# FP4 feed-forward and phazor convolution: the block scales of h computed on ScalarE, the shifts moved behind the next maxima, the sums ahead of the next up

## The chip, the cores and the metric

One core of a Trainium2 chip. The metric is the device time of one launch in microseconds (us). Engines are named as in the profile: PE (TensorE), ACT (ScalarE), DVE (VectorE), POOL (GpSimd), SP (SyncE).

## What is computed

x is 4 x 1024 x 128 in f32. With xn = layernorm(x) over the last axis, the result is

```
x + conv(xn) + ffn(xn)

conv:  y[t] = Re( gate * ( sum over s <= t of phazor^(t-s) * init * xn[s]  +  last * phazor^(t+1) ) )
ffn:   q(h) @ q(w_down).T   with  h = silu(q(xn) @ q(w_gate).T) * (q(xn) @ q(w_up).T)

q(v), blockwise over 16 elements of the last axis:
    scale = max( max|v| / 6, 1e-12 )
    q     = nearest of 0, .5, 1, 1.5, 2, 3, 4, 6 to |v|/scale, * sign(v) * scale
```

The hidden width is 352, so a row of h has 22 blocks and a row of xn has 8. The reference does the convolution by FFT; the kernel does it as a recurrence in time, one channel to a partition.

## The kernel before, in words

The 4096 rows are 32 tiles of 128 rows. Four tiles make a **group of x** g (8 groups), two tiles make a **pair** q (16 pairs, two to a group). x is quantised, transposed and convolved by group; h is made, quantised and multiplied by w_down by pair.

Every engine has a queue written out by hand, and the engines meet by semaphores only. The queues are in order: an instruction that waits holds all behind it. The names below are those of the code and of the rest of the text.

For pair q of h: PE does gate_tile for each tile (L769, one PSUM bank, so each gate waits for the silu of the tile before) and up_pair (L778, into slot q % 2 of ps_u). ACT does silu (L622). DVE then does product (L959), maxima of the blocks (amax_h, L963), the scales (L974), their inverses (L977) and the divide (L982), in place in PSUM. ACT takes the absolute value times 2^22 (big_h, L632). DVE rounds by two subtractions, shift_h (L987) and shift_back_h (L994, into hn). POOL multiplies by the scales (scale_h, L452, into hq), PE turns it (turn_h, L790), ACT copies it (copy_hT, L628), and PE sums x, the convolution and the product with w_down into ps_o (sum_parts L800 to L803, sum_down L811). ACT copies the sum out (copy_out, L636) and SP stores it.

For group g of x: ACT normalises four tiles (L590), DVE takes the maxima (x_amax, L945). From group 3 on they lie next to those of h of the even pair q = 2(g - 2), so that one instruction makes both kinds of scales (76 columns instead of 44). POOL divides (divide_x, L386), ACT makes big_x in two steps (L597, L602), POOL shifts, shifts back and scales (L391, L396, L401), PE turns the quantised x (turn_xq) and the plain xn (turn_xn), and ACT copies both (copy_xqT L615, copy_xnT L609). POOL multiplies xn by two tables (demodulate_re, demodulate_im, L424), DVE scans each (L1008: the real part in the even pair, the imaginary part in the odd one, in pair 1 and pair 14 both kinds as the code below says), and POOL multiplies the scanned states by two tables (modulate_re, modulate_im, L439, into y_re and y_im). Between the two groups of a batch entry ACT turns the state by four one-column activations (turn_state, L553 to L559). A scan reads a column that lies in the bank of the next pair's up, so it waits for the first tile of up_pair(q + 1).

Before the loop ACT has made the sine tables, has gone through copy_xnT(0) and the big values of w_down, and DVE has done the statistics of the first two groups of x; those of the other six follow the divide of pair 0 on DVE, and normalise(2) on ACT waits for them.

DVE's order in pair q was shift_h(q-1), shift_back_h(q-1), product(q), amax_h(q), x_amax, scales(q), inverses(q), divide_h(q), scan. The scales and the inverses count up one semaphore together (s_rc, two to a pair). up_pair(q) waits for the shift back of pair q - 2, whose slot it takes.

## Time and profile before

| | us |
|---|---|
| median of 3 runs | 149.05 (148.79 to 150.4) |
| the profiled execution, its time | 150.65 |
| the profiled execution, its span | 148.6 |
| DVE busy | 125.8 (85%) |
| POOL busy | 113.5 (76%) |
| PE busy | 112.2 (76%) |
| ACT busy | 94.3 (63%) |

The span reaches from the first to the last instruction of the execution that the profiler recorded; the time of the same execution also holds what lies around it, 2.05 us. The runs are timed without a profile. Busy time counts the instructions that work, not semaphores or waits. A row of the order of time has the start from the span's beginning, the length, the engine, the line of the code, the operation with what it writes and reads, how many like instructions are merged in it, and in brackets the idle time ahead of it, where there is any of note, with the engine and line that ended it.

### The profile page before, as it was taken

Reading aid. Unit: us, or ns where it says so; the run is one execution under the profiler, and the core shown is the slowest. Engines: PE = TensorE matmul, PEld = TensorE weight load, DVE = VectorE, ACT = ScalarE, POOL = GpSimd, SP = SyncE. Lnnn points to the kernel's source line nnn. Section 1 sums busy time; section 2 is a strip of 40 time slices with the busy share of each in tenths; the row PEclk is TensorE's granted clock in tenths of the full one; section 3 lists DMA queues with packets and bytes.
Section 4 is the critical chain, followed back from the end, with each engine's and each line's share of the span. In section 5 each row is a group of like instructions: output and inputs, shape, how many; then the busy total and the mean of one; then the engine's idle time right before and its main releaser. Section 6 shows DMA issues by size and latency. Waiting matters only on the chain. (4 is left out here: it accounts for less than half of the span.)

```text
span 148.6 us, 2137 instructions
## 1 busy us (share of the span) xinstructions
PE 112.2 (76%) x649; PEld 88.0 (59%) x649; DVE 125.8 (85%) x222; ACT 94.3 (63%) x197; POOL 113.5 (76%) x130
## 2 busy tenths in 40 slices
PE   4405988206867459998996999699979999985883
PEld 4305644103534448785885878486757868674873
DVE  0999939999599893899999999999999999999900
ACT  3866449993596548668886774888485456641422
POOL 3677865659959999989996999799799954935300
PEclk9965599855589999999999999999999999999599
DMA  5970000000000000100010010001001000101011
GB/s 152 295 273 0 0 2 0 0 0 2 2 4 0 0 0 0 71 0 4 0 71 0 0 71 7 0 2 71 0 4 46 24 0 0 71 4 67 3 35 35
DMA packets 2890, 4.90 MB, mean 33 GB/s; under 512 B 448, under 2 KB 832, under 8 KB 2880
## 3 DMA queue, kind: packets, MB, share of 16 engines
q1 hardware_dynamic: 2736, 4.77, 9.2%
q8 instruction: 5, 0.08, 0.2%
q14 instruction: 5, 0.04, 0.1%
q10 hardware_dynamic: 144, 0.00, 0.1%
HBM read 2.67 MB, written 2.10 MB: 32 GB/s over the span
## 5 line engine op out<-in xcount | busy, mean ns | idle before, releaser
L769 PE MATMUL ps_g<-wg_T,xq_T 128*128 128x352 f32 x64 | 27.7, 517 | 10.4 <-ACT silu L622 10.4
L811 PE MATMUL ps_o<-wd_T,hq_T 128*128 128x128 f32 x180 | 25.7, 280 | 0.0
L811 PEld LDWEIGHTS ps_o<-wd_T,hq_T 128*128 128x128 f32 x180 | 23.5, 199 | 0.0
L778 PE MATMUL ps_u<-wu_T,xq_T 128*128 128x352 f32 x64 | 23.0, 483 | 0.0
L622 ACT ACTIVATE silu<-ps_g 128x352 f32<-128x352 f32 x32 | 14.7, 460 | 12.9 <-PE ps_g L769 12.9
L452 POOL TENSOR_TENSOR hq<-hn,den 128x704 f32<-128x704 bf16 x15 | 20.8, 1387 | 2.0 <-PE ps_o L811 1.6
L632 ACT ACTIVATE big<-ps_u 128x704 bf16<-128x704 f32 (+1 forms) x17 | 12.2, 720 | 14.9 <-DVE ps_u L982 14.9
L769 PEld LDWEIGHTS ps_g<-wg_T,xq_T 128*128 128x128 f32 x64 | 10.5, 202 | 16.0 <-ACT silu L622 13.8
L790 PEld LDWEIGHTS ps_h<-ident,hq 128*128 128x128 f32 x96 | 12.6, 145 | 10.4 <-issue 5.3
L790 PE MATMUL ps_h<-ident,hq 128*128 128x128 f32 x96 | 16.2, 279 | 2.7 <-POOL hq L452 1.5
L628 ACT COPY hq_T<-ps_h 128x384 f32<-128x384 f32 x32 | 15.2, 474 | 4.4 <-PE ps_h L790 4.4
L959 DVE TENSOR_TENSOR ps_u<-silu,ps_u 128x704 f32<-128x704 f32 x16 | 14.2, 889 | 2.4 <-ACT silu L622 2.4
L439 POOL TENSOR_TENSOR y_re<-g_re,out_re 128x512 f32<-128x512 f32 x8 | 10.1, 1267 | 7.6 <-DVE g_re L1008 7.6
L987 DVE SCALAR_TENSOR_TENSOR ps_u<-big,ps_u 128x704 f32<-128x704 bf16 (+1 forms) x17 | 14.1, 835 | 1.5 <-ACT big L632 1.4
L982 DVE TENSOR_TENSOR ps_u<-ps_u,inv 128x704 f32<-128x704 f32 (+1 forms) x17 | 14.4, 855 | 0.6
L590 ACT ACTIVATE xn<-x_all,shift,rstd 128x128 f32<-128x128 f32 x32 | 13.6, 489 | 2.0 <-DVE shift L915 2.0
L963 DVE TENSOR_REDUCE ps_u<-ps_u 128x44 f32<-128x704 f32 x16 | 14.4, 899 | 0.5
L994 DVE SCALAR_TENSOR_TENSOR hn<-big,ps_u 128x704 bf16<-128x704 bf16 (+1 forms) x17 | 14.3, 843 | 0.5
L778 PEld LDWEIGHTS ps_u<-wu_T,xq_T 128*128 128x128 f32 x64 | 11.6, 199 | 5.0 <-issue 1.0
L800 PE MATMUL ps_o<-x_all,ident 128*128 128x128 f32 x60 | 12.2, 286 | 2.6 <-POOL y_im L439 1.9
L391 POOL TENSOR_TENSOR xt<-xbig,xv 128x512 f32<-128x512 f32 (+1 forms) x9 | 10.4, 1154 | 4.8 <-ACT xbig L602 4.8
L724 PE MATMUL ps_o<-ident 128*128 128x128 f32 x32 | 7.0, 408 | 9.4 <-ACT w_big L570 7.3
(145 smaller groups left out, 259.7 us busy)
## 6 DMA issues: line engine op xcount, KB each, us to landing
x_all<-x_in SPq DMA_DIRECT2D x8, 256.0 KB, 6.0
out<-x_all SPq DMA_DIRECT2D x7, 256.0 KB, 2.0
w_raw<-w_in SPq DMA_DIRECT2D x1, 560.0 KB, 5.5
out<-x_all SPq DMA_DIRECT2D x1, 128.0 KB, 1.7
out<-x_all SPq DMA_DIRECT2D x2, 64.0 KB, 1.5
par<-params_in ACTq DMA_DIRECT2D x1, 3.5 KB, 3.0
```

The costliest lines, as they stand in the source:

```text
L452: pool.tensor_tensor(hq_blocks(q), hn_blocks(q), pair_scales(den[q % 4]), ALU.mult).then_inc(s_hq, 1)
L622: act.activation(silu[q % 2][:, j, :], ps_g[:, 0:I], ACT.Silu).then_inc(s_silu, 1)
L628: act.copy(hq_T[t % 3][:, :], ps_h[:, 0:NCH * P]).then_inc(s_hTc, 1)
L769: pe.matmul(ps_g[:, 0:I], x_cols(t), wg_T[:, :], start=True, stop=True).then_inc(s_gate, 1)
L778: pe.matmul(slot(q)[:, j, 0:I], x_cols(q * PAIR + j), wu_T[:, :], start=True, stop=True).then_inc(s_up, 1)
L790: m = pe.transpose(ps_h[:, c * P:(c + 1) * P], hq[q % 3][:, j, CUT[c]:CUT[c] + P], ident[:, :])
L811: m = pe.matmul(o, hq_T[t % 3][:, c * P:(c + 1) * P], wd_T[:, c, :], start=False, stop=(c == NCH - 1))
L959: dve.tensor_tensor(in_slot(q), silu[q % 2][:, :, :], in_slot(q), ALU.mult).then_inc(s_h, 1)
L963: dve.tensor_reduce(maxima(q)[:, 0:HBP].rearrange("p (j b) -> p j b", b=HB), slot_blocks(q), X_AXIS, ALU.max, apply_absolute_value=True).t ...
L982: dve.tensor_tensor(slot_blocks(q, j0, j1), slot_blocks(q, j0, j1), pair_scales(inv[q % 2], j0, j1), ALU.mult).then_inc(s_hv, 1)
L987: dve.scalar_tensor_tensor(in_slot(q, j0, j1), big[q % 2][:, j0:j1, :], FLOOR, in_slot(q, j0, j1), ALU.max, ALU.subtract).then_inc(s_ht, 1)
L994: dve.scalar_tensor_tensor(hn[q % 3][:, j0:j1, :], big[q % 2][:, j0:j1, :], FLOOR, in_slot(q, j0, j1), ALU.max, ALU.subtract).then_inc(s_h ...
```

## The change

The scale of each block leaves DVE. ACT computes it in two activations: Relu(max * NUDGE/6 - TINY*NUDGE) into a new tile `above`, and Identity(above + TINY*NUDGE) into den, which together are the max of the two. They have semaphores of their own (s_above, s_den), and the inverses on DVE wait for s_den; s_rc now counts one to a pair. POOL sets two more constant columns.

On ACT the call scales(q) stands: for pair 0 behind big_down(); in even pairs behind turn_state and ahead of copy_xqT; in odd pairs behind copy_xnT and ahead of normalise. On DVE both shifts of the pair ahead move behind the maxima of the pair, ahead of the inverses. On POOL shift_back_x moves up to right behind shift_x, ahead of scale_h, and demodulate_re(g) moves from the end of the odd pair into the next even pair, ahead of modulate_im(g - 1). On PE up_pair(q + 1) moves from ahead of the sums of the pair to behind them, except for q = 0.

```diff
@@ DVE, the loop
             for q in range(NP):
                 g = q // 2
+                product(q)
+                amax_h(q)
+                if with_x(q):
+                    x_amax(g + 2, maxima(q)[:, X_COLS])
                 if q > 0:
                     shift_h(q - 1, 0, 0, PAIR)
                     shift_back_h(q - 1, 0, 0, PAIR)
-                product(q)
-                amax_h(q)
                 if q == 1:
                     scale_of_first_x(2)
-                if with_x(q):
-                    x_amax(g + 2, maxima(q)[:, X_COLS])
-                scales(q, with_x(q))
+                inverses(q, with_x(q))
                 divide_h(q)
@@ DVE, scales() becomes inverses()
-            def scales(q, x):
+            def inverses(q, x):
                 n = HBP + (XBG if x else 0)
-                dve.wait_ge(s_ham, q + 1)
+                dve.wait_ge(s_den, q + 1)
                 if x:
-                    g = q // 2 + 2
-                    dve.wait_ge(s_xam, g + 1)
-                    dve.wait_ge(s_xv, x_done(g - 1))
-                    dve.wait_ge(s_xq, x_done(g - 2))
-                dve.tensor_scalar(den[q % 4][:, 0:n], maxima(q)[:, 0:n], NUDGE / 6, TINY * NUDGE, ALU.mult,
-                                  ALU.max).then_inc(s_rc, 1)
-                dve.wait_ge(s_rc, 2 * q + 1)
+                    dve.wait_ge(s_xv, x_done(q // 2 + 1))
                 dve.reciprocal(inv[q % 2][:, 0:n], den[q % 4][:, 0:n]).then_inc(s_rc, 1)
@@ ACT, new
+            def scales(q):
+                n = HBP + (XBG if with_x(q) else 0)
+                act.wait_ge(s_ham, q + 1)
+                if with_x(q):
+                    g = q // 2 + 2
+                    act.wait_ge(s_xam, g + 1)
+                    act.wait_ge(s_xq, x_done(g - 2))
+                act.activation(above[:, 0:n], maxima(q)[:, 0:n], ACT.Relu, scale=NUDGE / 6,
+                               bias=neg_tiny_c).then_inc(s_above, 1)
+                act.wait_ge(s_above, q + 1)
+                if q >= 4:
+                    act.wait_ge(s_hq, q - 3)
+                act.activation(den[q % 4][:, 0:n], above[:, 0:n], ACT.Identity, bias=tiny_c).then_inc(s_den, 1)
@@ ACT, its places
             copy_xnT(0)
             big_down()
+            scales(0)
             big_h(0, 0, 0, PAIR)
...
                     if g % HALVES:
                         turn_state(g - 1)
+                    scales(q)
                     if g + 1 < NG:
                         copy_xqT(g + 1, 1, 0, GT)
...
                     if g + 1 < NG:
                         copy_xnT(g + 1)
+                    scales(q)
                     if g + 3 < NG:
@@ POOL
                     elif g > 0:
+                        demodulate_re(g)
                         modulate_im(g - 1)
                     if g > 0:
                         demodulate_im(g)
...
                         if g + 2 < NG:
                             shift_x(g + 2, 1, 0, GT)
+                            shift_back_x(g + 2, 1, 0, GT)
                     scale_h(q - 1)
                     if g == 0:
                         divide_x(2, 1, 0, GT)
                         demodulate_re(1)
                         shift_x(2, 1, 0, GT)
+                        shift_back_x(2, 1, 0, GT)
                     if g + 2 < NG:
-                        shift_back_x(g + 2, 1, 0, GT)
                         scale_x(g + 2, 1, 0, GT)
-                    if 0 < g < NG - 1:
-                        demodulate_re(g + 1)
@@ PE
-                if q < LAST:
-                    up_pair(q + 1)
+                if q == 0:
+                    up_pair(1)
                 if q in (0, 2):
                     turn_xq(q // 2 + 1, 1, 0, GT)
                 if q >= 2:
...
                     sum_parts(b, out_cols(b))
                     sum_down(b, out_cols(b))
+                if 0 < q < LAST:
+                    up_pair(q + 1)
```

## Rows read from the trace of the kernel before

**Rows 1.** Part 1 of the page: busy time, share and instructions of each engine.
```profile
PE 112.2 (76%) x649; PEld 88.0 (59%) x649; DVE 125.8 (85%) x222; ACT 94.3 (63%) x197; POOL 113.5 (76%) x130
```

**Rows 2.** Order of time on DVE, pairs 6 and 7: start, length, engine, line, operation.
```profile
74.99 0.89 DVE L959 TENSOR_TENSOR ps_u<-silu,ps_u 128x704 f32<-128x704 f32 x1
75.91 0.90 DVE L963 TENSOR_REDUCE ps_u<-ps_u 128x44 f32<-128x704 f32 x1
76.72 0.68 DVE L945 TENSOR_REDUCE ps_u<-xn 128x32 f32<-128x512 f32 x1
77.50 0.24 DVE L974 TENSOR_SCALAR den<-ps_u 128x76 f32<-128x76 f32 x1
77.77 0.63 DVE L977 RECIPROCAL inv<-den 128x76 f32<-128x76 f32 x1
78.43 0.90 DVE L982 TENSOR_TENSOR ps_u<-ps_u,inv 128x704 f32<-128x704 f32 x1
79.24 1.27 DVE L1008 TENSOR_TENSOR_SCAN g_re<-ps_u,turned,u_re 128x512 f32<-128x512 f32 x1
80.43 0.87 DVE L987 SCALAR_TENSOR_TENSOR ps_u<-big,ps_u 128x704 f32<-128x704 bf16 x1
...
82.14 0.89 DVE L959 TENSOR_TENSOR ps_u<-silu,ps_u 128x704 f32<-128x704 f32 x1
...
88.41 0.89 DVE L959 TENSOR_TENSOR ps_u<-silu,ps_u 128x704 f32<-128x704 f32 x1
```

**Rows 3.** Order of time on ACT, same stretch.
```profile
72.21 0.76 ACT L632 ACTIVATE big<-ps_u 128x704 bf16<-128x704 f32 x1 [0.46 <-DVE ps_u L982]
...
76.71 0.57 ACT L615 COPY xq_T<-ps_x 128x512 f32<-128x512 f32 x1
...
79.36 0.76 ACT L632 ACTIVATE big<-ps_u 128x704 bf16<-128x704 f32 x1 [1.30 <-DVE ps_u L982]
80.02 0.62 ACT L597 ACTIVATE xsq<-xv 128x512 f32<-128x512 f32 x1
...
81.30 0.44 ACT L622 ACTIVATE silu<-ps_g 128x352 f32<-128x352 f32 x1
...
84.29 0.89 ACT L590 ACTIVATE xn<-x_all,shift,rstd 128x128 f32<-128x128 f32 x2
```

**Rows 4.** Groups of ACT by form: count, then busy time and mean ns of one.
```profile
L556 ACT ACTIVATE turned<-g_re,turned,cos_t 128x1 f32<-128x1 f32 x4 | 1.5, 379 | 0.0
...
L602 ACT ACTIVATE xbig<-xsq,consts 128x256 f32<-128x256 f32 x2 | 1.0, 509 | 0.1
```

**Rows 5.** Order of time on POOL, same stretch.
```profile
74.56 1.28 POOL L439 TENSOR_TENSOR y_im<-g_im,out_im 128x512 f32<-128x512 f32 x1
...
77.02 1.39 POOL L452 TENSOR_TENSOR hq<-hn,den 128x704 f32<-128x704 bf16 x1
78.47 1.06 POOL L386 TENSOR_TENSOR xv<-xn,inv 128x512 f32<-128x512 f32 x1
```

**Rows 6.** Order of time on PE, same stretch: sums of two tiles, and what follows them.
```profile
76.81 0.38 PE L800 MATMUL ps_o<-x_all,ident 128*128 128x128 f32 x2
...
79.07 0.60 PE L745 MATMUL ps_x<-ident,xn 128*128 128x128 f32 x4
```

**Rows 7.** Order of time on DVE: inverses of pair 0, divides of pairs 2 and 15.
```profile
24.53 0.43 DVE L977 RECIPROCAL inv<-den 128x44 f32<-128x44 f32 x1
...
47.97 0.90 DVE L982 TENSOR_TENSOR ps_u<-ps_u,inv 128x704 f32<-128x704 f32 x1
...
137.77 0.96 DVE L982 TENSOR_TENSOR ps_u<-ps_u,inv 128x352 f32<-128x352 f32 x2
```

**Rows 8.** Order of time on ACT at the start: big_h(0) and copy_xnT(1).
```profile
27.95 0.74 ACT L632 ACTIVATE big<-ps_u 128x704 bf16<-128x704 f32 x1
...
39.57 1.07 ACT L609 COPY xn_T<-ps_x 128x512 f32<-128x512 f32 x1
```

**Rows 9.** Order of time on PE at the end: sum_parts(28).
```profile
138.08 0.77 PE L800 MATMUL ps_o<-x_all,ident 128*128 128x128 f32 x2 [0.72 <-issue]
```

More of the change, by code:

```diff
@@ L77, in build @@
         ident = sb("ident", [P, P])
-        consts = sb("consts", [P, 4])
+        consts = sb("consts", [P, 6])
+        above = sb("above", [P, HBP + XBG])
         steps = sb("steps", [P, GT + 1], I32)
@@ L202, in build @@
         s_ham = sem("h_amax_ready")
+        s_above = sem("h_scales_above_tiny")
+        s_den = sem("h_scales_ready")
         s_rc = sem("h_inverses_ready")
@@ L236, in build @@
         first_re, first_im, neg_turn = col(18), col(19), col(20)
-        base_c, quarter_c, round_c, unround_c = (consts[:, n:n + 1] for n in range(4))
+        base_c, quarter_c, round_c, unround_c, tiny_c, neg_tiny_c = (consts[:, n:n + 1] for n in range(6))
         X_COLS = slice(HBP, HBP + XBG)
@@ L317, in _ @@
             pool.memset(ident[:, :], 0.0).then_inc(s_idz, 1)
-            for c, value in ((base_c, BASE), (quarter_c, math.pi / 2), (round_c, ROUND), (unround_c, -ROUND)):
+            for c, value in ((base_c, BASE), (quarter_c, math.pi / 2), (round_c, ROUND), (unround_c, -ROUND),
+                             (tiny_c, TINY * NUDGE), (neg_tiny_c, -TINY * NUDGE)):
                 pool.memset(c, value).then_inc(s_const, 1)
@@ L382, in divide_x @@
                 else:
-                    pool.wait_ge(s_rc, 4 * g - 6)
+                    pool.wait_ge(s_rc, 2 * g - 3)
                 if g >= 3:
@@ L519, in whole_turns @@
             def whole_turns():
-                act.wait_ge(s_const, 4)
+                act.wait_ge(s_const, 6)
                 act.wait_ge(s_turns, 1)
@@ L964, in amax_h @@
                                   X_AXIS, ALU.max, apply_absolute_value=True).then_inc(s_ham, 1)
-            def scales(q, x):
+            def inverses(q, x):
                 n = HBP + (XBG if x else 0)
-                dve.wait_ge(s_ham, q + 1)
+                dve.wait_ge(s_den, q + 1)
                 if x:
-                    g = q // 2 + 2
-                    dve.wait_ge(s_xam, g + 1)
-                    dve.wait_ge(s_xv, x_done(g - 1))
-                    dve.wait_ge(s_xq, x_done(g - 2))
-                dve.tensor_scalar(den[q % 4][:, 0:n], maxima(q)[:, 0:n], NUDGE / 6, TINY * NUDGE, ALU.mult,
-                                  ALU.max).then_inc(s_rc, 1)
-                dve.wait_ge(s_rc, 2 * q + 1)
+                    dve.wait_ge(s_xv, x_done(q // 2 + 1))
                 dve.reciprocal(inv[q % 2][:, 0:n], den[q % 4][:, 0:n]).then_inc(s_rc, 1)
             def divide_h(q):
-                dve.wait_ge(s_rc, 2 * q + 2)
+                dve.wait_ge(s_rc, q + 1)
                 for j0, j1 in parts(q):
```

## The prediction

> **What bounds the kernel now.** I read the page's busy line first: DVE is the busiest engine at 85%, PE and POOL follow at 76%, ACT at 63% [rows 1]. A share over the whole span doesn't say which engine sets the pace of a stretch, so next comes DVE's own order of time over one group of x (two pairs, q=6 and q=7). Its instructions follow each other with no idle bracket, and the group takes 88.41 - 74.99 = 13.42 us [rows 2]. DVE is the bound there. The reader is to see the steps from start to start, because they are what an instruction costs in a full queue: product 0.92, maxima 0.81, maxima of x 0.78, scales 0.27, inverses 0.66 (with x), divide 0.81, scan 1.19, both shifts 1.71 (80.43 to 82.14) [rows 2]. Then ACT in the same stretch, for how late it comes with what DVE will now need [rows 3], then what POOL and PE do around it [rows 5, 6], and last the start and the end, where the engines hand one chain from one to the other [rows 7 to 9].
>
> **Part 1, the scale leaves DVE.** Sixteen tensor_scalar go, each worth 0.27 us (77.50 to 77.77). The reduction in front of it, 0.68 long, stepped 0.78 because the scale waited for its result; the one of 0.90 whose follower doesn't wait stepped 0.81 (75.91 to 76.72) [rows 2]. The shift that now follows doesn't wait either: another 0.1 to 0.2, taken as 0.1. So DVE alone would need 0.37 less per pair: an even pair with x 7.15 - 0.37 = 6.78, an odd one 6.27 - 0.37 = 5.90, a group 12.7 us. That is the whole gain on offer, about 16 x 0.37 = 5.9 us.
>
> **Part 2, its price on ACT.** Two dependent activations of 44 or 76 columns with a pointer bias take its place. The trace has none of this form. The nearest are 379 ns for one column with pointer scale and bias, and 509 ns for 256 columns with a bias alone [rows 4]. Reading between them gives about 0.35 each, and with the wait of the second for the first 0.75 us for both; the bounds are 0.5 (two of 0.25, if pointers cost less here than in the 379) and 0.95 (two of 0.45, between the two rows, and their hand-over). The Trainium skill, "ScalarE: Activation LUTs", Rules for kernel authors, budgets about 0.3 us plus 0.83 ns per element, an estimate of 0.67 to 0.73 for the two.
> The cover for it is the 1.7 us of both shifts, if ACT is free by then. ACT's queue is in order, and scales(q) stands behind silu, the hT copies and, in odd pairs, copy_xnT(g+1). So I follow ACT from the end of a divide.
>
> **Part 3, the new order on DVE moves ACT later.** Before, divide(q-1) was followed by scan and both shifts, and only then product(q): ACT's big_h(q-1), which starts when the divide ends, ran 2.8 us ahead of product(q) (79.36 against 82.14) [rows 2, 3]. Now only the scan lies between, and big_h(q-1) starts 1.1 us ahead. Everything behind it on ACT comes 1.7 us later against DVE, and scales(q) is one of those things.
> Odd pair with big_x (q=3, 5, 7, 9, 11), time 0 at the start of divide(q-1): the divide ends at 0.90; big_h starts at 0.93 and holds ACT 0.66. big_x needs divide_x, which stands on POOL behind scale_h(q-2); and scale_h(q-2) needs the shift back of that pair, which now ends only right before inverses(q-1), at about -0.6. scale_h 1.39 and divide_x 1.06 follow (77.02, 78.47) [rows 5]: xv is ready at about 1.95. So big_x starts at 1.95 and not at 1.6; its two activations step 1.28 (80.02 to 81.30); from silu(2q+2) to the end of copy_xnT are 2.99 (81.30 to 84.29) [rows 3]; the two new activations 0.75. The scales are ready at 7.0. DVE would be there at 0.81 + 1.19 + 0.92 + 0.81 + 1.71 = 5.44. It waits 1.5 us. A group is then 12.7 + 1.5 = 14.2 to 14.3 us, against 13.42: **0.8 us more per group**, not 0.7 less. With the scales at 0.5 and no wait for xv it would be 13.7, with 0.95 14.5; all are above 13.42.
> Even pairs: ACT has copy_out, two silu, two hT copies and, for odd g, the four activations of turn_state ahead of scales(q). From big_h(5) to their end it took 4.5 (72.21 to 76.71) [rows 3], 5.3 with the scales, where DVE needs from the divide's end 1.1 + 0.92 + 0.81 + 0.7 + 1.71 = 5.2. Nothing to speak of with x; without x (q=14, with turn_state) 0.7.
>
> **Part 4, POOL and PE.** POOL gets demodulate_re in front of modulate_im, so y_im, which ended 0.85 us after product(6) began (74.56 + 1.28 - 74.99) [rows 2, 5], comes at about 2.9 if POOL has no slack; in a longer group POOL has it (demodulate_re runs while DVE waits), y_im comes at about 1.4 and the sums start at 2.3. They now go ahead of up: 2.26 us of PE work (76.81 to 79.07) [rows 6] before up(q+1) starts, at 4.5 after product(q); its first tile, which the scan waits for, is there at 5.2 and the scan wants it at 5.6. Covered by 0.4 us; costed at nothing. On the last groups (q=12 on), where there is no big_x, gate(2q+2) comes behind sums and up and holds silu(2q+2) about as long as big_x did, so there is no gain there either. A wait placed on ACT holds silu, and with it the gate tiles.
>
> **Part 5, the start, where the change is dearest.** In pair 0 the inverses started at 24.53, and the moments and statistics of the late x followed the divide without a gap [rows 7]. Now inverses(0) needs scales(0), which ACT reaches behind silu(3), copy_xnT(0) and big_down, at 27.95, where big_h(0) began [rows 8]. With 0.75 the scales are there at 28.70 and inverses(0) starts at 28.75: **4.2 us later**, bounds 4.0 and 4.4. No shift stands in pair 0 to cover it. Moments, statistics, normalise(2), turn_xn(1), the gates of pair 2 all stand behind it, so the whole kernel moves by 4.2.
> Pair 1: scales(1) stands behind copy_xnT(1), which started at 39.57, and steps 0.85: 40.42 in the old clock [rows 8], scales ready at 41.2, divide at 41.65, scan at 42.45. The scan of before waited for up(2) as well, and began 2.0 earlier; the shifts of pair 1 then come behind product(2) in the new order. Carried through to divide(2), which was at 47.97 [rows 7], it is 1.7 more.
> Pairs 2 to 6: up(3) stands behind the first sums, which need y_im(0). By the same bookkeeping the scan of pair 2 waits 3.6 us for it and inverses(3) 1.2 for ACT, while waits of before go, so that little of it is net. From divide(2) to divide(6) I get 31.7 us against 78.43 - 47.97 = 30.5 [rows 2, 7]: 1.2 more, of which 0.8 is the group of pairs 5 and 6.
> Pairs 7 to 12: three more groups, 3 x 0.8 = 2.5. Pairs 13 to 15: the same path by ACT without big_x, with gate behind sums and up, 1.1. **The end:** the shift back of pair 14 ends only 0.46 ahead of divide(15), and POOL does scale_h(14) and modulate_im(7) behind it, 1.39 + 1.28 [rows 5], so y_im comes 2.2 after the divide's start; the sums of the last tiles want it, and began 0.3 after it (138.08 against 137.77) [rows 7, 9]. That is 1.9 later, of which I take 0.7 as got back further down, where PE and the hT copies wait for each other in turn: 1.2, bounds 0 and 2.
> **Sum:** 4.2 + 1.7 + 1.2 + 2.5 + 1.1 + 1.2 = 11.9 us on the profiled execution: span 148.6 to 160.5, its time 150.65 to 162.5. The median of the runs is 1.6 below the profiled execution's time, so against 149.05 the forecast is **161**.
>
> **The rivals.** (a) ACT is ready in time from pair 2 on: silu and copies move up into the idle that ACT has today (63% busy [rows 1]), and only the start pays. Then 4.2 + 1.7 + 1.2 less 13 x 0.37 = 4.8: +2.3, about 151. For it: ACT has idle time in each group. Against it: that idle lies ahead of big_h, on the wrong side of the chain counted in part 3.
> (b) The change works throughout, pair 0 too: DVE stays the bound and 5.9 less up to 1.2 at the end comes off: 143 to 145. It needs ACT free for scales(0) 4 us before its queue got there [rows 8]. The Trainium skill, "Perfetto Trace Analysis", Optimizing Scalar/DVE Operations, speaks for (b): with DVE saturated, "offloading some work to Scalar (or even GPSIMD) may make sense". The trace bears out the premise (no DVE idle over 13.42 us), not that ACT's queue gets there in time.
> (c) Slower still: the sums ahead of up stop the scan of every even pair because y_im stays late. If y_im comes at 2.9 in each group, up's first tile is at 5.85 instead of 5.6: 0.25 a group, plus up to 0.6 where the gate behind them comes later than big_x, over 5 groups: +4, 165. It decides only if POOL doesn't get back its slack.
> (d) It does something else than it says: Relu swaps ACT's table. Two reloads a pair, at anything near a microsecond each, would be over 20 us. The Trainium skill, "ScalarE: Activation LUTs", Table sets, lists relu as filler in every set; no run here shows it yet, but Square, Identity, Abs, Sin and Silu already run in this kernel without a swap between them.
>
> **How the numbers follow.** Forecast 0.78; (a) 0.08; (b) 0.04; (c) 0.09; (d) 0.01. The unknown costs of the forecast: the steady groups between +0.3 and +1.1 each (-2.5, +1), start 4.0 to 4.4, pairs 2 to 4 -1.5 to +1, the end -1.2 to +0.8. Together 155.5 to 163.5; the range reaches to (c)'s lower part and stops short of (a): 155 to 164. One per cent (1.5 us) is about what a measurement of this kernel can tell from no change: faster than that 0.04, within it 0.04, slower 0.92.
>
> **What would show it.** Step by step: DVE idle ahead of the inverses of pair 0, released by ACT's second activation, 4.2 us; ahead of those of odd pairs from 3 to 11, 1 to 1.5 us each, with copy_xnT right ahead of the scales on ACT; none in even pairs with x; starts of products two pairs apart 14.2 us; activations of 0.3 to 0.4 us. It is wrong if the inverses of odd pairs start right behind the shift back, or if the group is under 13.4 us; if the price is right and the place wrong, the idle stands ahead of the scans, with up as releaser, and (c) has it.

## The result, and the profile after

168.52 us median (167.46 to 169.68) against 149.44 for the kernel before beside it: ratio 1.127, 95% interval 1.116 to 1.139. The change makes the kernel slower by 19 us; the forecast was 12, to 161 us, with a range of 155 to 164. The direction and the price of the steady groups came out as worked. Three stretches were priced too low, and the cause of the largest miss was not in the sum at all. In this text a time is the median of all timed executions, while a ratio and its interval leave out executions in a slower state (among them one of 384.92 us of e5 and one of 168.34 us of e7).

The page of the changed kernel: span, busy times, and the group of the inverses from part 5.

```profile
span 167.4 us, 2167 instructions
...
PE 116.0 (69%) x649; PEld 91.0 (54%) x649; DVE 126.9 (76%) x206; ACT 102.2 (61%) x229; POOL 113.9 (68%) x132
...
L994 DVE RECIPROCAL inv<-den 128x44 f32<-128x44 f32 (+1 forms) x16 | 7.8, 487 | 14.7 <-ACT den L650 14.7
```

DVE is busy 1.1 us longer than before (126.9 against 125.8 [rows 1]), although the scales have left it, and idle 17.7 us longer (40.5 against 22.8). 14.7 us of the idle time are waits of the inverses for ACT: 4.36 in pair 0, 3.25 in pair 1, 0.60 in pair 3, 1.4 in each of pairs 5, 7, 9 and 11, and 0.57 and 0.30 in pairs 13 and 14.

The divides on DVE, order of time, pairs 4, 12 and 15; pairs 2 and 6 stand in fences below (57.91, 91.87), those of before in [rows 2, 7].

```profile
77.77 0.90 DVE L999 TENSOR_TENSOR ps_u<-ps_u,inv 128x704 f32<-128x704 f32 x1
...
133.35 0.90 DVE L999 TENSOR_TENSOR ps_u<-ps_u,inv 128x704 f32<-128x704 f32 x1
...
153.73 0.96 DVE L999 TENSOR_TENSOR ps_u<-ps_u,inv 128x352 f32<-128x352 f32 x2
```

Against the kernel before (whose divides of pairs 0, 4 and 12 began at 24.99, 65.01 and 117.80) the divide of pair 0 comes 3.8 us later, that of pair 2 9.9, of pair 4 12.8, of pair 6 13.4, of pair 12 15.6, of pair 15 16.0, and the end 18.8. The forecast had 4.2, 5.9, 6.3, 7.1, 9.6, 10.7 and 11.9. So the misses lie between pairs 0 and 2 (6.2 lost, 1.7 forecast), between pairs 2 and 4 (2.8 lost, 0.4 forecast) and at the end (2.8 lost, 1.2 forecast). From pair 4 to pair 15 it went the other way: the changed kernel lost 3.2 where 4.4 were forecast.

**The start.** DVE's order of time, from the inverses of pair 0 to the shift column, and POOL's beside it.

```profile
28.31 0.43 DVE L994 RECIPROCAL inv<-den 128x44 f32<-128x44 f32 x1 [4.36 <-ACT den L650]
28.77 0.90 DVE L999 TENSOR_TENSOR ps_u<-ps_u,inv 128x704 f32<-128x704 f32 x1
...
32.88 0.18 DVE L930 TENSOR_SCALAR rstd<-var 128x24 int32<-128x24 int32 x1
33.09 1.20 DVE L933 TENSOR_TENSOR tmp<-rstd 128x24 f32<-128x24 f32 x1
34.33 1.19 DVE L934 SCALAR_TENSOR_TENSOR tmp<-tmp,var 128x24 f32<-128x24 f32 x1
...
37.65 0.18 DVE L934 SCALAR_TENSOR_TENSOR tmp<-tmp,var 128x24 f32<-128x24 f32 x1
...
39.60 1.19 DVE L936 SCALAR_TENSOR_TENSOR rstd<-tmp,rstd 128x24 f32<-128x24 f32 x1
40.82 0.18 DVE L938 SCALAR_TENSOR_TENSOR shift<-mean,rstd 128x24 f32<-128x24 f32 x1
```

```profile
32.99 1.26 POOL L368 TENSOR_TENSOR in_re<-terms 128x512 f32<-128x512 f32 x1 [4.65 <-ACT terms L543]
34.21 1.26 POOL L369 TENSOR_TENSOR in_im<-terms 128x512 f32<-128x512 f32 x1
...
39.49 1.26 POOL L428 TENSOR_TENSOR u_im<-xn_T,in_im 128x512 f32<-128x512 f32 x1
```

The inverses wait 4.36 us for ACT, as forecast. The steps of the statistics that follow take 0.18 us up to 33.09. From there seven of the ten that are left take 0.65 to 1.20, and each of the seven ends 0.03 to 0.05 us after an instruction of POOL: 33.09 + 1.20 = 34.29 against 32.99 + 1.26 = 34.25, then 34.33 + 1.19 = 35.52 against 34.21 + 1.26 = 35.47. From the divide to the end of the shift column it is 41.00 - 28.77 = 12.2 us; before it was 32.52 - 24.99 = 7.5. The kernel before had shown it once, in the last step, which met POOL's first table:

```profile
31.04 0.18 DVE L913 SCALAR_TENSOR_TENSOR rstd<-tmp,rstd 128x24 f32<-128x24 f32 x1
31.26 1.26 DVE L915 SCALAR_TENSOR_TENSOR shift<-mean,rstd 128x24 f32<-128x24 f32 x1
...
31.22 1.26 POOL L364 TENSOR_TENSOR in_re<-terms 128x512 f32<-128x512 f32 x1 [2.48 <-ACT terms L539]
```

0.18 for the step that ran alone, 1.26 for the one that began 0.04 us after POOL's. The statistics had just missed the table work; 3.8 us later they lay under it. The Trainium skill, "SBUF — State Buffer", Who interferes with whom, has the rule: a DVE instruction with two inputs in SBUF and a GpSimd (POOL) instruction that reads SBUF contend for a shared port pair that one holds for its whole length, and the other is fully blocked. The trace agrees in every step above: the steps that began before POOL's instruction kept their 0.18 us (37.65 against 37.66 on POOL), those that began after it waited for its end.

The stretch counts as busy time of DVE, so it hides in the busy share; only the order of time shows it.

**The steady groups.** DVE, pairs 7 to 9, and ACT in the odd pair between.

```profile
87.18 0.87 DVE L982 TENSOR_TENSOR ps_u<-silu,ps_u 128x704 f32<-128x704 f32 x1
...
91.21 0.62 DVE L994 RECIPROCAL inv<-den 128x76 f32<-128x76 f32 x1
91.87 0.90 DVE L999 TENSOR_TENSOR ps_u<-ps_u,inv 128x704 f32<-128x704 f32 x1
92.67 1.27 DVE L1025 TENSOR_TENSOR_SCAN g_re<-ps_u,turned,u_re 128x512 f32<-128x512 f32 x1
...
98.81 0.43 DVE L994 RECIPROCAL inv<-den 128x44 f32<-128x44 f32 x1 [1.42 <-ACT den L650]
...
101.28 0.87 DVE L982 TENSOR_TENSOR ps_u<-silu,ps_u 128x704 f32<-128x704 f32 x1
```

```profile
93.81 0.63 ACT L601 ACTIVATE xsq<-xv 128x512 f32<-128x512 f32 x1 [0.25 <-POOL xv L390]
...
95.10 0.44 ACT L626 ACTIVATE silu<-ps_g 128x352 f32<-128x352 f32 x1
...
97.21 1.13 ACT L613 COPY xn_T<-ps_x 128x512 f32<-128x512 f32 x1
98.09 0.33 ACT L645 ACTIVATE above<-ps_u,consts 128x44 f32<-128x44 f32 x1
98.45 0.33 ACT L650 ACTIVATE den<-above,consts 128x44 f32<-128x44 f32 x1
98.69 0.86 ACT L594 ACTIVATE xn<-x_all,shift,rstd 128x128 f32<-128x128 f32 x2
```

The group, from one product to that two pairs on, takes 101.28 - 87.18 = 14.10 us (14.2 forecast, 13.42 before [rows 2]). In the even pair the inverses follow without idle; in the odd one they wait 1.42 us for den, the second activation on ACT, right behind copy_xnT. From the start of the first activation to the end of the second are 98.45 + 0.33 - 98.09 = 0.69 us (0.75 forecast).

**The first sums.** PE's windows (the columns are named in the first line) and the scan of pair 2.

```profile
core 0: us, PE busy (x) PEld busy (x) DVE busy (x) ACT busy (x) POOL busy (x), PEclk, DMA share, GB/s
59.44:63.83 4.39, 4.39 (x20) 4.39 (x21) 0.00 (x0) 0.91 (x3) 3.57 (x3) 0.50 0.01 4
```

```profile
57.91 0.90 DVE L999 TENSOR_TENSOR ps_u<-ps_u,inv 128x704 f32<-128x704 f32 x1
65.31 1.28 DVE L1025 TENSOR_TENSOR_SCAN g_re<-ps_u,turned,u_re 128x512 f32<-128x512 f32 x1 [6.50 <-PE ps_u L799]
```

The sums of tiles 0 and 1 take 4.39 us at a granted clock of 0.50; in steady pairs they take 2.3 [rows 6], and the same first sums of the kernel before took 2.34 (50.39 to 52.73) at 1.00. PE had worked 0.72 us in the 4.51 us ahead of them. up(3) stands behind them, and the scan waits 6.50 us for it, where 3.6 were forecast.

**The end.** POOL and PE behind the divide at 153.73.

```profile
153.44 1.38 POOL L456 TENSOR_TENSOR hq<-hn,den 128x704 f32<-128x704 bf16 x1 [3.35 <-DVE hn L1011]
154.78 1.27 POOL L443 TENSOR_TENSOR y_im<-g_im,out_im 128x512 f32<-128x512 f32 x1
```

```profile
156.14 0.77 PE L821 MATMUL ps_o<-x_all,ident 128*128 128x128 f32 x2 [0.37 <-issue]
```

ACT: copy_hT(28), and big_h(15) behind it.

```profile
155.81 0.48 ACT L632 COPY hq_T<-ps_h 128x384 f32<-128x384 f32 x1 [3.00 <-PE ps_h L811]
156.19 0.83 ACT L636 ACTIVATE big<-ps_u 128x352 bf16<-128x352 f32 x2
```

scale_h(14) and y_im come as worked, y_im ends at 156.05, 2.3 us after the divide's start. But hT(28) comes late too, and big_h(15) on ACT stands behind its copy: it begins 2.5 us after the start of the divide, where before it began 0.6 after it (138.34 against 137.77). From the start of the last divide to the end of the span are 13.7 us against 10.8. The first tile's sums ran at half clock in both kernels; those of the second (from 159.05) run at half clock only in the changed one. What that costs by itself no run separates.

### The profile page after: what moved, and what is told of

It is laid out like the page before. It is cut to its first block, busy times and chain, and to the rows that moved or that the text cites. A ratio compares the mean times of both kernels' runs of the same rounds, so it can differ in the third digit from the quotient of the medians.

```text
span 167.4 us, 2167 instructions
## 1 busy us (share of the span) xinstructions
PE 116.0 (69%) x649; PEld 91.0 (54%) x649; DVE 126.9 (76%) x206; ACT 102.2 (61%) x229; POOL 113.9 (68%) x132
## 4 chain that ended last, share of the span: by engine, by line
PE 22%; DVE 22%; issue 20%; POOL 18%; ACT 15%; DMA 2%; POOLq 0%; ACTq 0%; DVEq 0%
PE ps_g L790 6%; PE ps_o L832 4%; ACT xn_T L613 3%; PE ps_u L799 3%; POOL xt L400 3%; POOL xt L395 3%; ACT silu L626 3%; POOL y_re L443 3%; POOL hq L456 2%; DVE bn L912 2%; DVE ps_u L999 2%; POOL u_im L428 2%; DVE rstd L936 2%; PE ps_o L821 2%; DMA par<-params_in 2%
## 5 line engine op out<-in xcount | busy, mean ns | idle before, releaser
L790 PE MATMUL ps_g<-wg_T,xq_T 128*128 128x352 f32 x64 | 27.8, 518 | 13.7 <-ACT silu L626 13.5
L832 PE MATMUL ps_o<-wd_T,hq_T 128*128 128x128 f32 x180 | 27.3, 292 | 0.0
L832 PEld LDWEIGHTS ps_o<-wd_T,hq_T 128*128 128x128 f32 x180 | 25.2, 211 | 0.0
L790 PEld LDWEIGHTS ps_g<-wg_T,xq_T 128*128 128x128 f32 x64 | 11.0, 202 | 20.5 <-ACT silu L626 16.9
L636 ACT ACTIVATE big<-ps_u 128x704 bf16<-128x704 f32 (+1 forms) x17 | 12.2, 722 | 14.0 <-DVE ps_u L999 14.0
L811 PE MATMUL ps_h<-ident,hq 128*128 128x128 f32 x96 | 16.8, 287 | 4.8 <-POOL hq L456 3.3
L994 DVE RECIPROCAL inv<-den 128x44 f32<-128x44 f32 (+1 forms) x16 | 7.8, 487 | 14.7 <-ACT den L650 14.7
L594 ACT ACTIVATE xn<-x_all,shift,rstd 128x128 f32<-128x128 f32 x32 | 13.5, 482 | 8.8 <-DVE shift L938 8.8
L766 PE MATMUL ps_x<-ident,xn 128*128 128x128 f32 x32 | 5.3, 292 | 15.4 <-ACT xq_T L619 15.4
L1004 DVE SCALAR_TENSOR_TENSOR ps_u<-big,ps_u 128x704 f32<-128x704 bf16 (+1 forms) x17 | 14.2, 843 | 2.0 <-ACT big L636 2.0
L799 PEld LDWEIGHTS ps_u<-wu_T,xq_T 128*128 128x128 f32 x64 | 12.2, 208 | 4.9 <-issue 1.5
L1011 DVE SCALAR_TENSOR_TENSOR hn<-big,ps_u 128x704 bf16<-128x704 bf16 (+1 forms) x17 | 14.2, 842 | 0.5
L821 PE MATMUL ps_o<-x_all,ident 128*128 128x128 f32 x60 | 12.9, 300 | 2.4 <-POOL y_im L443 1.9
```

The costliest lines, as they stand in the source:

```text
L790: pe.matmul(ps_g[:, 0:I], x_cols(t), wg_T[:, :], start=True, stop=True).then_inc(s_gate, 1)
L799: pe.matmul(slot(q)[:, j, 0:I], x_cols(q * PAIR + j), wu_T[:, :], start=True, stop=True).then_inc(s_up, 1)
L811: m = pe.transpose(ps_h[:, c * P:(c + 1) * P], hq[q % 3][:, j, CUT[c]:CUT[c] + P], ident[:, :])
L821: pe.matmul(o, ident[:, :], x_all[:, t, :], start=True, stop=False)
L832: m = pe.matmul(o, hq_T[t % 3][:, c * P:(c + 1) * P], wd_T[:, c, :], start=False, stop=(c == NCH - 1))
L1004: dve.scalar_tensor_tensor(in_slot(q, j0, j1), big[q % 2][:, j0:j1, :], FLOOR, in_slot(q, j0, j1), ALU.max, ALU.subtract).then_inc(s_ht, 1)
```

## The experiments

All but e6 start from the changed kernel. The ratios compare with the kernel before, run beside each experiment on the same chip; the microseconds that a run is said to gain are, unless another run is named, against the 168.52 of the changed kernel, timed separately beside a kernel before of 149.44. The place of the first instructions in the span differs from one profile to the next (the inverses of pair 0 of e8 to e13, all but e11, begin at 23.94 to 25.83), so lengths are taken within one profile. "The scan waits for up" means that it waits for the first tile of the next pair's up on PE.

**e1: scales of pair 0 on DVE.**

```diff
@@ DVE, pair 0 alone
+                if q == 0:
+                    scales(q, with_x(q))
                 inverses(q, with_x(q))
@@ ACT
-            scales(0)
```

scales(q, x) on DVE is the tensor_scalar of the kernel before, counting up s_den.

> The changed kernel, with the scales of pair 0 alone made on DVE as before. Theory A (the late scales cost twice: DVE waits 4.4 us for ACT, and the statistics, pushed under POOL's table work, stretch from 7.5 to 12.2 us from divide to shift column, because DVE's small instructions on two SBUF operands wait for each POOL instruction to end): the divide of pair 0 is back at about 25, the shift column ends at about 32.5, and with PE idle for 7 instead of 15 us its granted clock is back at full before the first sums; together 8.5 to 11 us less than the changed kernel, 157.5 to 160. Rival R1 (the stretch of the statistics has another cause than when they run): 4.2 us less, about 164.

159.51 us, ratio 1.064 (1.052 to 1.075): 9 us less, in the range of theory A. The divide of pair 0 is back at 24.90 and that of pair 1 at 41.50 (50.05 in the changed kernel), so the start cost about twice its wait. The hoped-for clock was not there: the granted clock from 47 to 54 us, in which the first sums begin, is 0.50, and the scan of pair 2 still waits 5.4 us.

**e2: POOL waits for the statistics.**

```diff
@@ POOL
             first_state()
+            pool.wait_ge(s_stats, 2)
             in_tables()
```

> The changed kernel, but POOL waits for the late statistics before it makes the in tables; DVE's late start stays. Theory A (POOL's instructions hold DVE's small ones): every step of the statistics is 0.2 us again, from the divide of pair 0 to the end of the shift column 7.5 us as in the kernel before, at most 6.5 without the stretch of the last one; POOL's tables come later, so the whole gains only 2 to 4.5 us: 164 to 166.5. Rival R1 (ACT's table terms, or the semaphore hand-over, stretch them): the steps stay at up to 1.2 us and the time at 168.5 or above it.

161.56 us, ratio 1.082 (1.073 to 1.092), 7 us less from one added wait: more than theory A said, which had counted on a loss by POOL's later tables. DVE's late start stays (divide of pair 0 at 28.43), and the steps are short:

```profile
32.75 0.18 DVE L934 TENSOR_TENSOR tmp<-rstd 128x24 f32<-128x24 f32 x1
...
34.70 0.18 DVE L939 SCALAR_TENSOR_TENSOR shift<-mean,rstd 128x24 f32<-128x24 f32 x1
```

The shift column ends at 34.88 instead of 41.00: from the divide 6.45 us instead of 12.23. The rest of the gain shows at the scan of pair 2, which waits 5.2 us for up instead of 6.5. Nothing on ACT or in DVE's own semaphores was changed, so POOL's instructions were what held DVE.

**e3: all scales on DVE, the other moves kept.**

```diff
@@ DVE, every pair
+                scales(q, with_x(q))
                 inverses(q, with_x(q))
@@ ACT
-            every call of scales(q)
```

> The changed kernel with the scales of all pairs on DVE (right ahead of the inverses, so that nothing waits for them), all the other moves kept. Theory A (ACT's in-order queue makes the odd pairs wait): no idle ahead of the inverses, group of x 12.7 + 0.5 = 13.2 to 13.4 us, start as in the kernel before; 150 to 154. Rival R2 (the moves of the shifts and of up cost by themselves, through silu and gate): the group stays near 14 us, the idle moves to the product or the scan; 156 to 159.

157.07 us, ratio 1.049 (1.039 to 1.059). No inverses wait, the start is that of before (12.81 us from divide to divide of pairs 0 and 1 in both), and yet it is 8 us slower than before: rival R2 had the time (156 to 159) and the place.

```profile
67.56 0.90 DVE L1008 TENSOR_TENSOR ps_u<-ps_u,inv 128x704 f32<-128x704 f32 x1
68.51 1.28 DVE L1034 TENSOR_TENSOR_SCAN g_re<-ps_u,vec,u_re 128x512 f32<-128x512 f32 x1
...
75.15 1.28 DVE L1034 TENSOR_TENSOR_SCAN g_im<-ps_u,vec,u_im 128x512 f32<-128x512 f32 x1 [0.41 <-PE ps_u L796]
...
81.31 0.90 DVE L1008 TENSOR_TENSOR ps_u<-ps_u,inv 128x704 f32<-128x704 f32 x1
```

The group is 81.31 - 67.56 = 13.75 us. The scans of odd pairs now wait for up behind the sums (0.41 in pair 5, 0.55 in the next ones; pair 4 loses 0.14, 0.95 from divide to scan instead of 0.81), and the scan of pair 2 waits 7.0.

**e4: scales of the odd pairs ahead of silu(2q+3) on ACT.**

```diff
@@ ACT, odd pairs
                         copy_hT(2 * q - 4)
+                    scales(q)
                     if q < LAST:
                         silu_tile(2 * q + 3)
...
                         copy_xnT(g + 1)
-                    scales(q)
```

> The changed kernel with scales(q) of the odd pairs moved on ACT ahead of silu(2q+3), where ACT waits for the gate anyway. Theory A: the 1.4 us of idle ahead of the inverses of odd pairs goes, but big_h then waits behind the normalise, so the group falls from 14.1 to between 13.0 and 13.5; 3 to 5 us less, 163.5 to 165.5. Rival R2 (the odd pairs are held by something else of the new order): group above 13.8, time within 1.5 of 168.5.

165.05 us, ratio 1.103 (1.092 to 1.113): the time is in theory A's range, the group is not. The waits of the odd inverses from pair 3 on are gone, and the group goes from 14.1 to 13.76 us (76.32 to 90.08), where theory A named 13.0 to 13.5. The scans take over: that of pair 4 waits 0.3 us for up, that of pair 5 0.7, and those of pairs 7, 9 and 11 wait 1.07. Of the shorter wait of the inverses of pair 1 (0.30 instead of 3.25) little comes through: counted from the divide of pair 0, that of pair 4 is 1.2 us earlier.

**e5: up(3) ahead of the first sums.**

```diff
@@ PE
-                if q == 0:
-                    up_pair(1)
+                if q in (0, 2):
+                    up_pair(q + 1)
```

> The changed kernel, with up_pair(3) alone back ahead of the first sums on PE. Theory A (the 6.5 us that the scan of pair 2 waits are those sums, which wait for y_im(0) and then run at half the granted clock, and gate(8) stands behind up(3) too): the wait of that scan falls under 1 us; the inverses of pair 3 then wait for ACT, which needs the divide of x from POOL first, so 2.5 to 3.5 us less in all: 165 to 166. Rival R3 (all of the wait is net loss): 6 us less, 162.5. Rival R4 (the wait is of no account, the den of pair 3 ends later anyway): within 1 of 168.5.

167.10 us, ratio 1.119 (1.110 to 1.128): 1.4 us less, between the ranges of theory A and of rival R4. The same kernel in one more execution, for its waits:

> The kernel of e5 once more for one look at its waits. As in e5: the scan of pair 2 waits under 1 us, the inverses of pair 3 for ACT, span about 165.

Span 163.6, time 165.55. The scan of pair 2 waits for nothing, the inverses of pair 3 wait 3.2 us for ACT, and the divide of pair 4 comes at 74.88 instead of 77.77. So of a wait of 6.5 us 1.4 (by the medians) to 2.9 (by this divide) were net loss.

**e6: the kernel before with up behind the sums.** The same move on PE as in the change, nothing else.

```diff
@@ PE
-                if q < LAST:
-                    up_pair(q + 1)
+                if q == 0:
+                    up_pair(1)
...
                     sum_down(b, out_cols(b))
+                if 0 < q < LAST:
+                    up_pair(q + 1)
```

> The kernel before with the move on PE alone: up_pair(q+1) behind the sums for q > 0. Theory A: nothing in the steady groups (DVE still 13.42 a group), but the scan of pair 2 waits for the first sums, some 5 to 6 us where it waited for nothing, of which later waits of the kernel before (3.3 us) give part back: 151.5 to 154.5. Rival R3: the scans of the steady pairs wait too, 0.5 us or more in each, and the time is over 156.

155.29 us, ratio 1.042 (1.034 to 1.051): 6 us by this move alone, between theory A and rival R3.

```profile
55.06 1.28 DVE L1010 TENSOR_TENSOR_SCAN g_re<-ps_u,turned,u_re 128x512 f32<-128x512 f32 x1 [6.76 <-PE ps_u L778]
```

The scan of pair 2 waits 6.8 us, and the group of pairs 5 and 6 is 81.54 - 67.69 = 13.85 instead of 13.42, with scans of odd pairs waiting 0.3: theory A, which had nothing in the steady groups, was wrong there.

**e7: the shifts of pair 14 ahead of product(15).**

```diff
@@ DVE
+                if q == LAST:
+                    shift_h(q - 1, 0, 0, PAIR)
+                    shift_back_h(q - 1, 0, 0, PAIR)
                 product(q)
```

> The changed kernel, with both shifts of pair 14 ahead of the product of pair 15 as before, the rest of the order kept. Theory A (the 2.8 us that the end got longer behind the divide of pair 15 are scale_h(14) coming late, with copy_hT(28) and so big_h(15) behind it on ACT): the stretch from the last divide to the end goes back from 13.7 to about 11 us; the last divide itself comes up to 0.5 later: 1.8 to 2.8 us less, 165.7 to 166.7. Rival: the end is long because PE's clock is low there, and the time doesn't move by more than 0.7.

165.65 us, ratio 1.109 (1.100 to 1.118), 2.9 less: the rival is out. big_h(15) begins 0.6 us after the divide again. The last divide comes 0.6 later, and the stretch from it to the end is 12.1 instead of 13.7, not the 11 of theory A, in a profiled execution that was itself 2.7 us above this kernel's median. In it the sums of the last tiles run at half clock as well.

**e11: PE kept at work ahead of the first sums.**

```diff
@@ PE, q == 2
+                    pe.wait_ge(s_wTc, 3)
+                    warm(ps_o, 14)
                     turn_xq(2, 1, 0, GT)
+                    warm(ps_o, 14)
```

> The changed kernel, with 28 transposes of the identity on PE in pair 2, in the two stretches in which it waits for xq and for y_im ahead of the first sums. Theory A (those sums take 4.3 us instead of 2.3 because PE had stood idle and runs them at half its clock): they take 2.3 to 2.6, the granted clock of the stretch is near 1.0, the scan of pair 2 waits 4.3 to 4.8 instead of 6.5 us, and 1.3 to 2.2 us come off the time: 166.3 to 167.2. Rival: the sums take as long as before, or the extra work delays them; time 168.5 or more.

167.05 us, ratio 1.113 (1.105 to 1.120).

```profile
core 0: us, PE busy (x) PEld busy (x) DVE busy (x) ACT busy (x) POOL busy (x), PEclk, DMA share, GB/s
59.42:61.76 2.34, 2.34 (x21) 2.34 (x22) 0.00 (x0) 0.15 (x1) 2.34 (x2) 1.00 0.00 0
```

Theory A holds. The same sums take 2.34 us at a granted clock of 1.00 instead of 4.39 at 0.50, the scan waits 3.8 us instead of 6.5 (3.6 were forecast), and the divide of pair 4 comes 2.6 us earlier. That is what the forecast lacked between pairs 2 and 4 (2.4 us), so the clock accounts for it; by the medians the whole kernel gains 1.5 us.

**e8: the waiting places mended together.** Pairs 0, 1 and 15 make their scales on DVE, up(3) and the shifts of pair 14 as in e5 and e7, and on ACT in odd pairs silu(2q+2), a hT copy, big_x, silu(2q+3), scales(q) in this order.

```diff
@@ ACT, odd pairs (and scales(0) away, as in e1)
-                    elif g + 2 < NG:
-                        big_x(g + 2, 1, 0, GT)
...
                         copy_hT(2 * q - 4)
+                    if q > 1 and g + 2 < NG:
+                        big_x(g + 2, 1, 0, GT)
                     if q < LAST:
                         silu_tile(2 * q + 3)
+                    if 1 < q < LAST:
+                        scales(q)
...
-                    scales(q)
@@ DVE
+                if q in (0, 1, LAST):
+                    scales(q, with_x(q))
                 inverses(q, with_x(q))
```

> All places that waited are mended, with the scales of pairs 2 to 14 on ACT: pairs 0, 1 and 15 make theirs on DVE, up_pair(3) is ahead of the first sums, the shifts of pair 14 are in the old place, and on ACT in odd pairs silu(2q+2) and a hT copy go ahead of big_x, and scales(q) behind silu(2q+3). Theory A (the idea is sound where ACT gets there in time): the group of x falls to 12.8 to 13.2 us, the start and the end are those of before, 146 to 149. Rival R2 (ACT's chain of big_h, big_x, silu, copies and normalise is itself longer than DVE's queue now): the group stays at 13.4 or more, 150 to 153.

155.53 us, ratio 1.044 (1.034 to 1.054), group 14.49 us: theory A missed, and R2, which had the group at 13.4 or more, missed the time (150 to 153) and named ACT, where the waits are for PE and POOL. PE, POOL and DVE around the scan of pair 4:

```profile
61.34 0.60 PE L774 MATMUL ps_x<-ident,xv 128*128 128x128 f32 x4
63.35 0.46 PE L821 MATMUL ps_o<-x_all,ident 128*128 128x128 f32 x2 [1.41 <-issue]
...
61.97 1.28 POOL L443 TENSOR_TENSOR y_im<-g_im,out_im 128x512 f32<-128x512 f32 x1
...
66.53 1.28 DVE L1037 TENSOR_TENSOR_SCAN g_re<-ps_u,vec,u_re 128x512 f32<-128x512 f32 x1 [1.08 <-PE ps_u L799]
```

xq is turned at 61.34 and PE then waits 1.4 us for y_im, which ends at 63.25; up stands behind those sums, and the scan of the even pair waits 1.08 for it. POOL has u_re (demodulate_re) ahead of y_im, as rival (c) of the prediction had it. The inverses of pairs 2 and 3 still wait 1.1 and 3.0 us for ACT.

**e9: e8 with modulate_im(g-1) ahead of demodulate_re(g).**

```diff
@@ POOL
-                        demodulate_re(g)
                         modulate_im(g - 1)
+                        demodulate_re(g)
```

> The mended kernel (e8), with modulate_im(g-1) back ahead of demodulate_re(g) on POOL. Theory C (the mended kernel fell on rival (c): its POOL is late, y_im comes behind u_re, the sums wait 1.4 us for it, up stands behind the sums and the scans wait 1.1 and 0.6 us for up): the scan of even pairs waits for nothing, the group of x falls from 14.5 to 13.0 to 13.6 us, the time from 155.5 to 149 to 152. Rival: another wait ends last at nearly the same time (hT copies ahead of the sums, or POOL's own load), the group stays above 14.

149.40 us, where the kernel before took 150.35 beside it, ratio 0.997 (0.991 to 1.003): 6 us less than e8 from the order of two POOL instructions, as theory C had it. Scans of even pairs wait for nothing, those of odd ones 0.6; the group is 13.27.

**e10: as e9, big_x first and scales ahead of silu(2q+3).**

```diff
@@ ACT, odd pairs
+                    elif g + 2 < NG:
+                        big_x(g + 2, 1, 0, GT)
...
                         copy_hT(2 * q - 4)
-                    if q > 1 and g + 2 < NG:
-                        big_x(g + 2, 1, 0, GT)
-                    if q < LAST:
-                        silu_tile(2 * q + 3)
                     if 1 < q < LAST:
                         scales(q)
+                    if q < LAST:
+                        silu_tile(2 * q + 3)
```

> As e9, but with ACT's old order in odd pairs, big_x ahead of silu(2q+2), and scales(q) ahead of silu(2q+3). Theory A: big_x early keeps POOL ahead, but silu and so gate, sums and up come 1.3 us later; the scans of odd pairs wait about 1 us for up as in e4, group 13.6 to 13.9, time 150.5 to 153. Rival: with y_im early the scans wait less and the group is 13.2 or under, time under 149.

152.70 us, ratio 1.015 (1.007 to 1.023), group 13.75, and the scans of odd pairs wait 1.1 us for up, all as theory A has it.

**e12: as e9, pairs 2 and 3 on DVE too.**

```diff
@@ DVE (and scales of these pairs away on ACT)
-                if q in (0, 1, LAST):
+                if q in (0, 1, 2, 3, LAST):
                     scales(q, with_x(q))
```

> The kernel of e9 with the scales of pairs 2 and 3 on DVE as well, so that ACT makes them in pairs 4 to 14 only. Theory A: the waits of those two pairs for ACT (1.1 and 2.8 us in e9) go, the steady group stays at 13.27: 1.5 to 3 us less than e9, 146.5 to 148. Rival: pair 3 then waits for silu or for up instead, and the time is that of e9, 149 to 150.

150.22 us, ratio 1.002 (0.996 to 1.007): the rival. Counted from the inverses of pair 0, those of pair 3 come 3.6 us earlier than in e9 (28.92 instead of 32.47), and its scan then waits 3.8 us for up.

**e13: as e12, the second hT copy of odd pairs ahead of the scales.**

```diff
@@ ACT, odd pairs
-                    if 3 < q < LAST:
-                        scales(q)
                     if q >= 2:
                         copy_hT(2 * q - 3)
+                    if 3 < q < LAST:
+                        scales(q)
```

> As e12, with the second hT copy of the odd pairs ahead of the scales on ACT. Theory A (the scans of odd pairs wait 0.6 us for up because the sums ahead of it wait for that copy): the wait for up goes and one of up to 0.4 us for the scales comes; group 13.0 to 13.3, within 1 us of e12. Rival: the scales are now late again by more than the copy was, group over 13.4, 1 to 2 us more than e12.

148.73 us, where the kernel before took 148.97 beside it, ratio 0.996 (0.991 to 1.001), as theory A has it. DVE, pairs 5 to 8:

```profile
70.25 0.43 DVE L1007 RECIPROCAL inv<-den 128x44 f32<-128x44 f32 x1 [0.27 <-ACT den L650]
...
77.44 0.90 DVE L1012 TENSOR_TENSOR ps_u<-ps_u,inv 128x704 f32<-128x704 f32 x1
78.51 1.28 DVE L1038 TENSOR_TENSOR_SCAN g_re<-ps_u,turned,u_re 128x512 f32<-128x512 f32 x1 [0.17 <-PE ps_u L800]
...
90.66 0.90 DVE L1012 TENSOR_TENSOR ps_u<-ps_u,inv 128x704 f32<-128x704 f32 x1
```

Even scans wait 0.2 for up, odd inverses 0.3 for ACT. The group is 90.66 - 77.44 = 13.22 us, 0.2 less than before where 0.7 was on offer. In these 13.22 us DVE is busy for 12.57, PE for 12.33, POOL for 12.14 and ACT for 11.09; in the 13.42 of the kernel before it was 13.02, 11.99, 12.22 and 10.38.

## Why the prediction was wrong, step by step

The way the change acts was worked out rightly for the steady groups, and the sum failed at the start: it took work that was moved to a later time to keep its length. Two smaller terms, the first sums and the end, were mis-sized too.

- **Direction and steady groups: right.** Part 3 holds: the moved shifts make big_h and all behind it on ACT late, the odd inverses wait (1.5 forecast, 1.4 measured), the even ones don't. 3.3 was forecast from divide 4 to 12 against 2.8 measured. The price of the two activations was 0.69 for 0.75.
- **Part 5, pair 0: the wait right, what follows wrong.** "Moments, statistics, normalise(2), ... stand behind it, so the whole kernel moves by 4.2" took the statistics to keep their length wherever they run. They grew by 4.7 us under POOL's tables (12.2 for 7.5), shown by e2. This is the step that failed: a cost of moving work against another engine, absent from the sum. What is left between pairs 0 and 2, 6.2 - 4.7 = 1.5 us, is the 1.7 that was forecast.
- **Pairs 2 to 4: 2.8 for 0.4.** The bookkeeping of part 5 took the first sums at 2.26 us, the length of [rows 6], measured at full clock. They run at half of it and take 4.39; e11 shows what that costs, 2.6 us at the divide of pair 4. The forecast did name the place of the wait and its releaser.
- **The end: 2.8 for 1.2.** The 0.7 that I took as got back was not, and big_h(15) behind copy_hT(28) on ACT was left out. e7, with the shifts of pair 14 in the old place, takes 2.9 us off the time, but in its profile only 1.6 off this stretch: the late shifts are the larger part of the cause, and the rest stays open.
- **Pairs 12 to 15: 0.4 for 1.1.** Oversized: the waits there were 0.4 (scan of pair 12), 0.6 (inverses of pair 13) and 0.3 (pair 14), and the lighter queue of DVE gave most of it back. This error and that of the steady groups, 1.2 us together, made the whole miss smaller: that is luck.
- **Part 4, up behind the sums "costed at nothing".** True inside the changed kernel, whose scans in steady pairs don't wait, because its groups are long. In the order of before the move costs 0.4 us a group and 6 us in all (e6). A cover that holds only because something else is slow is no cover for the mended kernel. These 6 us are most of the 8 by which e3 stayed behind the kernel before; the other 2 were not taken apart, since no run makes the move of the shifts alone.
- **Rivals.** (a) and (b) did not come; (d) neither, no table load was added to the two of the start. (c) did not come in the changed kernel, but its mechanism is real: it is what held e8.
- **The gain on offer, 0.37 us a pair, stays mostly unearned** even with all mended (e9, e12, e13: the time of before within 0.5%). At about 13.2 us a group the scans wait for up, which waits for sums, hT copies and silu in turn, and DVE, PE and POOL are each busy for over 12 of the 13.22 us of e13. That several engines are at their limit at once is read from these waits and busy times and not shown; no run took PE's load down to prove it.

## What to carry to other kernels

Before a block of many small instructions is delayed, look at what the other engines run at the time to which it moves: same instruction, same engine, 0.18 or 1.2 us. When work is taken off the bound engine onto an in-order queue, follow that queue from the event that starts it, with all that stands ahead; free time in its busy share says nothing about being free at the right moment. A moved matmul stretch is priced at the clock that it will meet there, not at that of the row it is copied from.

## What the runs showed of the hardware

- Small DVE instructions with both inputs in SBUF wait for a running POOL tensor_tensor to end: 0.18 us alone, up to 1.26 under it, with ends 0.03 to 0.05 us after POOL's. The same step with POOL held back (e2) is 0.18 again. A small tensor_scalar with one input in SBUF (den_x, 128x32 f32) did the same: 0.26 us in the kernel before, 0.87 at 45.09 in the changed one, where it ended 0.03 us after scale_h(0) on POOL. DVE's large instructions with one input in PSUM keep their 0.87 to 0.90 us beside a busy POOL in every steady group.
- PE's first sums took 4.39 us at a granted clock of 0.50 after a stretch with little work (0.72 us in 4.51), and 2.34 at 1.00 when transposes filled the stretch (1.2 and 2.4 GHz are the two levels).
- Relu on 44 columns from PSUM with a pointer bias (a constant column in SBUF) is 0.28 to 0.33 us, Identity with one 0.33 (76 columns: 0.32 and 0.36). They stand between silu and copies, and the trace has no table load but the two ahead of the main work, as before (1.28 us each).
